# The later batches' layer-norm rows normalised on GpSimd instead of VectorE

## The chip, the cores and the metric

The kernel runs on one core of a Trainium2 chip. The metric is the device time of that core in microseconds. A core has five engines with a queue of instructions each: TensorE (PE in the rows; PEld is its weight load), VectorE (DVE), ScalarE (ACT), GpSimd (POOL) and SyncE (SP), which here only issues DMAs.

## The reference

Four batches of 512 rows by 512 columns go through an attention-like mixer and a feed-forward block, each behind a layer norm and with a residual. Cut to what is computed:

```
_layernorm(x) = (x - mean(x)) / sqrt(var(x) + 1e-5)

q, kv = (n @ W_q.T), (n @ W_kv.T)            # n = _layernorm(x), 16 heads of 32
qf, kvf = fft(q), fft(kv)                    # along each head
qf, kvf = qf / |qf|, kvf / |kvf|             # L2 norm of each head
kvf = cumsum(kvf, axis=1)                    # along the 512 rows of a batch
x = x + (ifft(qf * kvf).real @ W_o.T)

n2 = _layernorm(x)
gate = silu((n2 @ fp8(gate_w)) * gate_scale) # 512 -> 1536
up   = (n2 @ fp8(up_w)) * up_scale           # 512 -> 1536
x = x + ((gate * up) @ fp8(down_w)) * down_scale
```

## The kernel before, in words

A batch b (0 to 3) is four tiles t of 128 rows by 512 columns. The Fourier matrices are folded into the projection weights once. To keep precision with 16-bit matmuls, an activation is stored as a high part and a low part (the value less its high part), and both go through TensorE.

The first norm of a tile has these steps: `dve_stats1` (mean and variance), `dve_root0_head`, `act_root0`, `dve_root0_tail` (the factor 1/sqrt, for four tiles at once), `dve_xn` (line 1074: row less mean, times factor, a TENSOR_SCALAR of 128x512 f32 with two per-partition scalars, into one of two buffers `xn`), `act_xh` (line 653, the high part into `xs`), `pool_xl` (line 1603, the low part), and `sp_xT` (line 1709), two DMA transposes into `xT`. TensorE then runs `pe_qk(b, t, 0)` and `pe_qk(b, t, 1)` (line 370), 12 matmuls each.

The second norm: `dve_o` (residual and statistics), `dve_ln2_head`, `act_sqrt2`, `dve_ln2_tail` (four short instructions that end on semaphore `v_n2`), `dve_hn` (line 1213, the same form of TENSOR_SCALAR, into `qk[:, t, 1, :]`), `act_hT` (line 731, high part into `ks`), `dve_hT` (line 1218, low part), and `sp_hT` (line 1722), two DMA transposes into `hT`. `pe_gate_up(b, 0)` (line 470) waits for all eight transposes of its batch.

Every engine's order is written out by hand and an engine never passes a waiting instruction. The work of batch b's feed-forward block is interleaved with the mixer of batch b+1. On TensorE, `pe_qk(b+1, ...)` for seven of eight pieces stands at the seam between two feed-forward blocks, just ahead of `pe_gate_up(b, 0)`. The eight pieces of `pe_qk` share two PSUM banks in turn, so `pe_qk(2, 1, 0)` can't start until ScalarE has read the bank of `pe_qk(2, 0, 0)` (`act_qk`, lines 667 and 675; its last reader counts `a_cp`). The two buffers of `xs` are freed by the transposes that read them: `act_xh(b, t)` waits for the landing of tile t-2.

`dve_f` (line 1234) is the feed-forward's product of gate and up, `dve_fu` (line 1241) its low part.

ScalarE's order at the seam ahead of batch 1's feed-forward block, and SyncE's, are:

```
act_fu(e, 11)
act_hT(e, 1, 0) ... act_hT(e, 1, 3)
act_xh(e, 2, 3)
act_qk(e, 2, 0, 0)

sp_hT(e, 1, 1); sp_xT(e, 2, 3); sp_hT(e, 1, 2); sp_hT(e, 1, 3); sp_hT(e, 1, 0)
```

The rest, with the line numbers of the profile:

Of the kernel before, what the change touches and what calls it, by code (L numbers as in the profile page):

```python
# [10 lines left out]
ALU = mybir.AluOpType  # L11
# [4 lines left out]
NB = 4  # L16
NT = 4
# [74 lines left out]
def build(nc, x, w_q, w_kv, woT, gate_w, up_w, down_w, gs_d, us_d, ds_d, cst_d, cst2_d, id_d, out):  # L92
    ctx = ExitStack()
    with ctx:
# [3 lines left out]
        def sem(name):  # L98
            return ctx.enter_context(nc.semaphore(name))
# [61 lines left out]
        def bank(name):  # L161
# [136 lines left out]
        def xs_free(e, b, t):  # L298

            if 4 * b + t > 1:  # L300
                was_b, was_t = divmod(4 * b + t - 2, NT)
                e.wait_ge(d_xT[was_t], 32 * (was_b + 1))

        def x_low_done(b, t):
            return (v_xl, 1) if (b, t) == (0, 0) else (p_xl, 4 * b + t)
# [342 lines left out]

        def act_xh(e, b, t):

            e.wait_ge(v_xn, 4 * b + t + 1)
            xs_free(e, b, t)
            e.activation(xs[:, t % 2, 0, :], xn[:, t % 2, :], ACT.Copy).then_inc(a_xh, 1)  # L653

# [68 lines left out]

        def act_hT(e, b, t):

            e.wait_ge(v_hn, 4 * b + t + 1)
            if b == 0:
                e.wait_ge(s_tri, 4)
            else:
                e.wait_ge(d_zT[t], 32 * b)  # L730
            e.activation(ks[:, 0, t, :], qk[:, t, 1, :], ACT.Copy).then_inc(a_hT, 1)
# [549 lines left out]
        def vector_program(e):  # L1281
# [131 lines left out]
            dve_product(e, 1, 1)  # L1413
            dve_zl(e, 1, 0)
            dve_scale(e, 1, 2, 0)
            dve_xn(e, 2, 0)
            dve_f(e, 5)
            dve_round(e, 11)
            dve_fu(e, 4)
            dve_xn(e, 2, 1)  # L1420
            dve_round(e, 12)
            dve_f(e, 6)
            dve_scale(e, 1, 3, 1)
# [19 lines left out]
            dve_zl(e, 1, 3)  # L1443
            dve_o(e, 1, 1)
            dve_f(e, 11)
            dve_xn(e, 2, 2)
            dve_round(e, 17)
            dve_o(e, 1, 2)
            dve_fu(e, 10)
            dve_o(e, 1, 3)  # L1450
            dve_ln2_head(e, 1, range(NT))
            dve_ln2_tail(e, 1, range(NT))
            dve_hn(e, 1, 0)
            dve_hn(e, 1, 1)
            dve_hn(e, 1, 2)
            dve_xn(e, 2, 3)
# [7 lines left out]
            for b in range(1, NB):  # L1464
                nxt = b + 1
                if nxt < NB:
                    dve_sum(e, nxt, 0, 0)
                    dve_sum(e, nxt, 0, 1)
                if nxt == HALF:
                    dve_most(e, 0, 0)  # L1470
                if nxt < NB:
                    dve_sum(e, nxt, 1, 0)
                if nxt == HALF:
                    dve_most(e, 0, 1)
                if nxt < NB:
                    dve_sum(e, nxt, 1, 1)
                if nxt == HALF:
                    dve_most(e, 1, 0)
                if nxt < NB:
                    dve_sum(e, nxt, 2, 0)  # L1480
                if nxt == HALF:
                    dve_most(e, 1, 1)
                    dve_most(e, 2, 0)
                    dve_most(e, 2, 1)
                    dve_gus(e)
                dve_f(e, b * NI)
                dve_scale_out(e, b - 1, 0)
                dve_fu(e, b * NI)
                if nxt < NB:
                    dve_sum(e, nxt, 2, 1)  # L1490
                dve_scale_out(e, b - 1, 1)
                if nxt < NB:
                    dve_sum(e, nxt, 3, 0)
                dve_scale_out(e, b - 1, 2)
                dve_scale_out(e, b - 1, 3)
                if nxt < NB:
                    dve_sum(e, nxt, 3, 1)
                dve_f(e, b * NI + 1)
                if nxt < NB:
                    dve_norm_tail(e, nxt, range(NT))  # L1500
                    dve_scale(e, nxt, 0, 1)
                if b + 2 < NB:
                    dve_stats1(e, b + 2, 0)
                dve_fu(e, b * NI + 1)
                if nxt < NB:
                    dve_scale(e, nxt, 0, 0)
                    dve_scale(e, nxt, 1, 1)
                dve_f(e, b * NI + 2)
                if nxt < NB:
                    dve_product(e, nxt, 0)  # L1510
                dve_f(e, b * NI + 3)
                if nxt < NB:
                    dve_scale(e, nxt, 1, 0)
                dve_fu(e, b * NI + 2)
                if nxt < NB:
                    dve_zl(e, nxt, 0)
                    dve_scale(e, nxt, 2, 1)
                dve_f(e, b * NI + 4)
                if nxt < NB:
                    dve_scale(e, nxt, 2, 0)  # L1520
                    dve_product(e, nxt, 1)
                    dve_scale(e, nxt, 3, 1)
                dve_fu(e, b * NI + 3)
                if nxt == HALF:
                    dve_unit2(e)
                if nxt < NB:
                    dve_zl(e, nxt, 1)
                    dve_product(e, nxt, 2)
                dve_f(e, b * NI + 5)
                if nxt < NB:  # L1530
                    dve_o(e, nxt, 0)
                dve_fu(e, b * NI + 4)
                if nxt < NB:
                    dve_scale(e, nxt, 3, 0)
                dve_f(e, b * NI + 6)
                dve_fu(e, b * NI + 5)
                if nxt < NB:
                    dve_product(e, nxt, 3)
                    dve_zl(e, nxt, 2)
                    dve_zl(e, nxt, 3)  # L1540
                    dve_o(e, nxt, 1)
                    dve_o(e, nxt, 2)
                dve_f(e, b * NI + 7)
                if nxt < NB:
                    dve_o(e, nxt, 3)
                    dve_ln2_head(e, nxt, range(NT))
                dve_fu(e, b * NI + 6)
                if nxt < NB:
                    dve_ln2_tail(e, nxt, range(NT))
                    dve_hn(e, nxt, 0)  # L1550
                dve_f(e, b * NI + 8)
                if nxt < NB:
                    dve_hT(e, nxt, 0)
                if b + 2 < NB:
                    dve_stats1(e, b + 2, 1)
                if nxt < NB:
                    dve_hn(e, nxt, 1)
                dve_fu(e, b * NI + 7)
                if b + 2 < NB:
                    dve_stats1(e, b + 2, 2)  # L1560
                if nxt < NB:
                    dve_hn(e, nxt, 2)
                    dve_hT(e, nxt, 1)
                if b + 2 < NB:
                    dve_stats1(e, b + 2, 3)
                if nxt < NB:
                    dve_hn(e, nxt, 3)
                    dve_hT(e, nxt, 2)
                dve_f(e, b * NI + 9)
                if nxt < NB:  # L1570
                    dve_hT(e, nxt, 3)
                dve_fu(e, b * NI + 8)
                if b + 2 < NB:
                    dve_root0_head(e, b + 2, range(NT))
                dve_fu(e, b * NI + 9)
                if b + 2 < NB:
                    dve_root0_tail(e, b + 2, range(NT))
                    dve_xn(e, b + 2, 0)
                    dve_xn(e, b + 2, 1)
                dve_f(e, b * NI + 10)  # L1580
                dve_fu(e, b * NI + 10)
                if b + 2 < NB:
                    dve_xn(e, b + 2, 2)
                dve_f(e, b * NI + 11)
                dve_fu(e, b * NI + 11)
                if b + 2 < NB:
                    dve_xn(e, b + 2, 3)
            for t in range(3):
                dve_scale_out(e, NB - 1, t)
            dve_out_half(e)  # L1590
# [50 lines left out]
        def gpsimd_program(e):  # L1641
# [18 lines left out]
            pool_ks(e, 1, 1)  # L1660
            pool_product(e, 1, 0)
            pool_ks(e, 1, 2)
            pool_xl(e, 2, 0)
            pool_product(e, 1, 1)
            pool_product(e, 1, 2)
            pool_ks(e, 1, 3)
            pool_product(e, 1, 3)
            pool_xl(e, 2, 1)
            pool_xl(e, 2, 2)
            pool_xl(e, 2, 3)  # L1670

            for b in range(1, NB):
# [8 lines left out]
                if nxt < NB:  # L1681
# [5 lines left out]
                    pool_product(e, nxt, 2)  # L1687
                    pool_ks(e, nxt, 3)
                    pool_product(e, nxt, 3)
                if b + 2 < NB:  # L1690
                    pool_xl(e, b + 2, 0)
                    pool_xl(e, b + 2, 1)
                    pool_xl(e, b + 2, 2)
                    pool_xl(e, b + 2, 3)
            pool_out(e, NB - 1, 0)
# [245 lines left out]
```

## Time and profile before

| | us |
|---|---|
| median of 3 runs | 420.11 (420.07 to 420.39) |
| the profiled execution, its own time | 419.79 |
| its span, first to last instruction | 418.0 |
| TensorE busy | 408.8 (98% of the span) |
| VectorE busy | 297.4 (71%) |
| ScalarE busy | 193.2 (46%) |
| GpSimd busy | 108.2 (26%) |

The mean granted TensorE clock is 0.996 of full speed. The profile is of one execution; the 1.8 us between its time and its span lie outside the instructions. Its page gives busy time by engine and a chain of waits followed back from the last instruction. The share of that chain is 89% TensorE, 3% DMA, 3% VectorE, 2% ScalarE, 1% GpSimd.

### The profile page before, as it was taken

Reading aid. Unit: us, or ns where it says so; the run is one execution under the profiler, and the core shown is the slowest. Engines: PE = TensorE matmul, PEld = TensorE weight load, DVE = VectorE, ACT = ScalarE, POOL = GpSimd, SP = SyncE. Lnnn points to the kernel's source line nnn. Section 1 sums busy time; section 2 is a strip of 40 time slices with the busy share of each in tenths; the row PEclk is TensorE's granted clock in tenths of the full one; section 3 lists DMA queues with packets and bytes.
Section 4 is the critical chain, followed back from the end, with each engine's and each line's share of the span. In section 5 each row is a group of like instructions: output and inputs, shape, how many; then the busy total and the mean of one; then the engine's idle time right before and its main releaser. Section 6 shows DMA issues by size and latency. Waiting matters only on the chain.

```text
span 418.0 us, 5504 instructions
## 1 busy us (share of the span) xinstructions
PE 408.8 (98%) x1897; PEld 202.8 (49%) x1897; DVE 297.4 (71%) x514; ACT 193.2 (46%) x323; POOL 108.2 (26%) x114
## 2 busy tenths in 40 slices
PE   7999999999999999999999999999999999999994
PEld 3744454445555554454555555454444444444442
DVE  4998998999999699997984972167865854422234
ACT  3687756587736245445242563255442441131220
POOL 0133551015154137043541012032461001300003
PEclk9999999999999999999999999999999999999998
DMA  8986546600181143232112014411112051200002
GB/s 249 264 267 239 163 117 162 149 17 2 38 256 36 26 77 71 57 127 74 28 26 50 2 29 101 72 50 53 26 26 52 0 77 25 100 2 0 2 0 101
DMA packets 57547, 33.55 MB, mean 80 GB/s; under 512 B 49456, under 2 KB 49840, under 8 KB 57392
## 3 DMA queue, kind: packets, MB, share of 16 engines
q1 hardware_dynamic: 57088, 32.93, 30.3%
q8 instruction: 15, 0.25, 0.3%
q10 hardware_dynamic: 432, 0.28, 0.2%
q14 instruction: 12, 0.10, 0.1%
HBM read 17.44 MB, written 4.19 MB: 52 GB/s over the span
## 4 chain that ended last, share of the span: by engine, by line
PE 89%; DMA 3%; DVE 3%; ACT 2%; POOL 1%; SPq 1%; issue 1%; POOLq 0%; DVEq 0%
PE bd L488 20%; PE bu L470 19%; PE bg L470 19%; PE ba L370 14%; PE ba L415 8%; PE bd L370 3%; DMA h<-x_dram 1%; PE ba L388 1%; PE bd L415 1%; DMA hT<-w_q_dram 1%; PE bd L388 1%; PE bd L356 1%; PE bu L415 1%; POOL xs L1603 1%; PE bg L447 0%
## 5 line engine op out<-in xcount | busy, mean ns | idle before, releaser
L470 PE MATMUL bu<-hT,gu 128*128 128x512 f16 x384 | 90.7, 379 | 0.0
L470 PE MATMUL bg<-hT,gu 128*128 128x512 f16 x376 | 89.0, 379 | 0.0
L1234 DVE SCALAR_TENSOR_TENSOR ff<-bu,us,sl 128x512 f32<-128x512 f32 x48 | 35.9, 748 | 56.0 <-PE bu L470 52.8
L741 ACT ACTIVATE sl<-bg,gs 128x512 f32<-128x512 f32 x48 | 32.9, 686 | 78.0 <-PE bg L470 77.0
L370 PE MATMUL ba<-wf,xT 128*128 128x512 f16 x288 | 63.2, 379 | 0.0
L470 PEld LDWEIGHTS bu<-hT,gu 128*128 128x128 f16 x384 | 37.5, 98 | 45.5 <-DVE ff L1234 0.6
L470 PEld LDWEIGHTS bg<-hT,gu 128*128 128x128 f16 x376 | 35.6, 98 | 44.9 <-issue 4.1
L488 PE MATMUL bd<-dw,fu 128*128 128x512 f32 x192 | 51.1, 411 | 0.0
L1634 POOL TENSOR_TENSOR h<-ff,h 128x512 f32<-128x512 f32 x14 | 17.5, 1272 | 122.2 <-DVE ff L1265 122.2
L370 PEld LDWEIGHTS ba<-wf,xT 128*128 128x128 f16 x288 | 27.9, 98 | 34.1 <-issue 1.1
L488 PE MATMUL bd<-own,half 128*128 128x512 f16 x184 | 43.0, 379 | 0.0
L1603 POOL TENSOR_TENSOR xs<-xn,xs 128x512 f16<-128x512 f32 x15 | 20.4, 1369 | 79.7 <-ACT xs L653 79.7
L488 PEld LDWEIGHTS bd<-dw,fu 128*128 128x128 f32 x192 | 36.1, 188 | 9.6 <-DVE fu L1241 0.4
L1616 POOL TENSOR_TENSOR ks<-qk,ks 128x512 f16<-128x512 f32 x16 | 21.2, 1325 | 48.8 <-ACT ks L704 48.8
L415 PE MATMUL ba<-wo,qk 128*128 128x512 f16 x144 | 32.6, 379 | 0.0
L1050 DVE TENSOR_REDUCE S<-tu 128x16 f32<-128x512 f32 x32 | 21.5, 676 | 11.2 <-ACT tu L667 11.2
L488 PEld LDWEIGHTS bd<-own,half 128*128 128x128 f16 x184 | 17.9, 98 | 21.9 <-DVE half L1241 0.6
L1241 DVE TENSOR_TENSOR half<-ff,half 128x512 f16<-128x512 f32 x23 | 19.3, 839 | 11.9 <-ACT half L747 11.7
L667 ACT ACTIVATE tu<-ba 128x512 f32<-128x512 f32 x24 | 14.3, 594 | 22.2 <-PE ba L370 22.2
L1139 DVE TENSOR_TENSOR qk<-qk,sc 128x512 f32<-128x512 f32 x32 | 23.0, 736 | 0.2
L1241 DVE TENSOR_TENSOR fu<-ff,fu 128x512 fp32r<-128x512 f32 x24 | 20.8, 872 | 3.2 <-ACT fu L747 3.0
L747 ACT ACTIVATE half<-ff 128x512 f16<-128x512 f32 x23 | 14.3, 623 | 18.4 <-PE bd L488 13.2
(201 smaller groups left out, 524.3 us busy)
## 6 DMA issues: line engine op xcount, KB each, us to landing
h<-x_dram SPq DMA_DIRECT2D x16, 256.0 KB, 4.2
out_dram<-h SPq DMA_DIRECT2D x15, 256.0 KB, 2.0
hT<-w_q_dram SPq DMA_DIRECT2D x4, 256.0 KB, 5.0
gu<-w_kv_dram SPq DMA_DIRECT2D x4, 256.0 KB, 4.4
hT<-gate_w_dram SPq DMA_DIRECT2D x2, 512.0 KB, 3.5
hT<-up_w_dram SPq DMA_DIRECT2D x2, 512.0 KB, 5.6
gu<-woT_dram SPq DMA_DIRECT2D x1, 1024.0 KB, 5.1
hT<-down_w_dram SPq DMA_DIRECT2D x2, 512.0 KB, 4.9
```

Source lines behind the costliest of these rows:

```text
L370: m = e.matmul(ba[i][:, :], xT[:, b % 2, part_x, k, P * t:P * t + P], wf[:, w, part_w, k, :], start=k == 0 and part_x == part_w, stop=k == ...
L415: m = e.matmul(ba[i][:, :], src[:, part_p, P * j:P * j + P], wo[:, part_w, j, :], start=j == 0 and part_p == part_w, stop=j == KT - 1 and ...
L470: m = e.matmul(bk[:, :], gu[:, c, 4 * w + k, col:col + P], hT[:, b % 2, part, k, :], start=k == 0 and part == 0, stop=k == KT - 1 and part ...
L488: m = e.matmul(bd[t][:, :], fu_at(n)[:, part, P * t:P * t + P], (dw if n < HALF * NI else dw16)[:, i, :], start=i == 0 and part == 0, stop ...
L741: e.activation(sl[:, n % 2, :], bg[:, :], ACT.Silu, scale=gs[:, i:i + 1]).then_inc(a_silu, 1)
L1050: e.tensor_reduce(S[:, t, NH * w:NH * w + NH], v, AX.X, ALU.add).then_inc(v_sum, 1)
L1139: e.tensor_tensor(split_heads(qk[:, t, w, :]), split_heads(qk[:, t, w, :]), head_scale(t, w), ALU.mult).then_inc(v_kn if w else v_qn, 1)
L1234: e.scalar_tensor_tensor(out=ff[:, n % 2, :], in0=bu[:, :], scalar=(us if b < HALF else us2)[:, i:i + 1], in1=sl[:, n % 2, :], op0=ALU.mul ...
L1241: e.tensor_tensor(fu_at(n)[:, 1, :], ff[:, n % 2, :], high.bitcast(F32) if n < HALF * NI else high, ALU.subtract).then_inc(v_fu, 1)
L1603: e.tensor_tensor(xs[:, t % 2, 1, :], xn[:, t % 2, :], xs[:, t % 2, 0, :], ALU.subtract).then_inc(p_xl, 1)
L1616: e.tensor_tensor(ks[:, 1, t, :], qk[:, t, 1, :], ks[:, 0, t, :], ALU.subtract).then_inc(p_ks, 1)
L1634: e.tensor_tensor(hh, y_at(b, t), hh, ALU.add).then_inc(p_out, 1)
```

## The change

`dve_xn` of batches 2 and 3 (8 pieces) and `dve_hn` of batches 1, 2 and 3 (12 pieces) leave VectorE. GpSimd does the same arithmetic with the same form of instruction, in `pool_xn` and `pool_hn`; ScalarE waits on GpSimd's semaphores for them. Batches 0 and 1 of the first norm and batch 0 of the second stay on VectorE.

```diff
+        def xn_done(b, t):
+            return (v_xn, 4 * b + t + 1) if b < 2 else (p_xn, 4 * (b - 2) + t + 1)
+
+        def hn_done(b, t):
+            return (v_hn, t + 1) if b == 0 else (p_hn, 4 * (b - 1) + t + 1)
...
         def act_xh(e, b, t):
 
-            e.wait_ge(v_xn, 4 * b + t + 1)
+            e.wait_ge(*xn_done(b, t))
...
         def act_hT(e, b, t):
 
-            e.wait_ge(v_hn, 4 * b + t + 1)
+            e.wait_ge(*hn_done(b, t))
...
+        def pool_xn(e, b, t):
+            e.wait_ge(v_r1, 2 * roots_of(b, t) + 2)
+            e.wait_ge(*x_low_done(*divmod(4 * b + t - 2, NT)))
+            e.tensor_scalar(xn[:, t % 2, :], h[:, b % 3, t, :], mv1[:, t, 0:1], E1[:, 2, t:t + 1], ALU.subtract,
+                            ALU.mult).then_inc(p_xn, 1)
+
+        def pool_hn(e, b, t):
+            e.wait_ge(v_n2, 5 * n1_of(b, t) + 5)
+            e.wait_ge(p_ks, 4 * b + NT)
+            e.tensor_scalar(qk[:, t, 1, :], h[:, b % 3, t, :], mv2[:, t, 0:1], E2[:, 4, t:t + 1], ALU.subtract,
+                            ALU.mult).then_inc(p_hn, 1)
...
             pool_ks(e, 1, 2)
+            pool_xn(e, 2, 0)
+            pool_product(e, 1, 1)
+            pool_xn(e, 2, 1)
             pool_xl(e, 2, 0)
-            pool_product(e, 1, 1)
...
             pool_xl(e, 2, 1)
+            pool_xn(e, 2, 2)
+            pool_xn(e, 2, 3)
             pool_xl(e, 2, 2)
+            pool_hn(e, 1, 0)
+            pool_hn(e, 1, 1)
+            pool_hn(e, 1, 2)
+            pool_hn(e, 1, 3)
             pool_xl(e, 2, 3)
```

On VectorE the calls are dropped where they stood. In the loop over b the four `pool_hn(nxt, t)` stand behind the mixer's last `pool_product`, and `pool_xn(b + 2, t)` between the calls of `pool_xl(b + 2, t)`.

GpSimd ahead of the first seam (the end of batch 0's feed-forward block), before; xs is the low part of a tile, own the 16-bit copy of the down weights:

```order
L1616 TENSOR_TENSOR ks<-qk,ks 128x512 [waits act_ks]
L1625 TENSOR_TENSOR qk<-tu 128x16x16 [waits dve_U]
L1626 TENSOR_TENSOR qk<-tu 128x16x16
L1629 COPY qk<-tu 128x32 [waits pool_im,pool_re]
L1603 TENSOR_TENSOR xs<-xn,xs 128x512 [waits d_xT3,act_xh]
L1603 TENSOR_TENSOR xs<-xn,xs 128x512 [waits d_xT0,act_xh]
L1603 TENSOR_TENSOR xs<-xn,xs 128x512 [waits d_xT1,act_xh]
L1608 CAST own<-dw 128x1024 [waits dve_rd]
```

The same place now (1603 is `pool_hn` here, 1592 the low part, 1597 `pool_xn`):

```order
L1617 TENSOR_TENSOR ks<-qk,ks 128x512 [waits act_ks]
L1626 TENSOR_TENSOR qk<-tu 128x16x16 [waits dve_U]
L1627 TENSOR_TENSOR qk<-tu 128x16x16
L1630 COPY qk<-tu 128x32 [waits pool_im,pool_re]
L1592 TENSOR_TENSOR xs<-xn,xs 128x512 [waits d_xT3,act_xh]
L1597 TENSOR_SCALAR xn<-h,mv,E 128x512 [waits pool_xl,dve_r1] x2
L1592 TENSOR_TENSOR xs<-xn,xs 128x512 [waits d_xT0,act_xh]
L1603 TENSOR_SCALAR qk<-h,mv,E 128x512 [waits pool_ks,dve_n2] x4
L1592 TENSOR_TENSOR xs<-xn,xs 128x512 [waits d_xT1,act_xh]
L1609 CAST own<-dw 128x1024 [waits dve_rd]
```

Four pieces of the second norm now stand ahead of the low part of tile 3 of batch 2, and the last two pieces of the first norm ahead of that of tile 2.

VectorE at the same seam, before, from the last step of `dve_ln2_tail` on:

```order
L1125 SCALAR_TENSOR_TENSOR E<-E 128x4
L1213 TENSOR_SCALAR qk<-h,mv,E 128x512 x3
L1074 TENSOR_SCALAR xn<-h,mv,E 128x512
L1218 TENSOR_TENSOR ks<-qk,ks 128x512
L1213 TENSOR_SCALAR qk<-h,mv,E 128x512
L1218 TENSOR_TENSOR ks<-qk,ks 128x512
L1241 TENSOR_TENSOR fu<-ff,fu 128x512
L1218 TENSOR_TENSOR ks<-qk,ks 128x512 x2
```

And now (1226 is `dve_hT`, 1249 `dve_fu`):

```order
L1133 SCALAR_TENSOR_TENSOR E<-E 128x4
L1226 TENSOR_TENSOR ks<-qk,ks 128x512 x2
L1249 TENSOR_TENSOR fu<-ff,fu 128x512
L1226 TENSOR_TENSOR ks<-qk,ks 128x512 x2
```

Five TENSOR_SCALAR are gone from this stretch, and the five TENSOR_TENSOR that follow each other now have their inputs from GpSimd by way of ScalarE.

## Rows read from the trace of the kernel before

**Rows 1.** Page, part 1: busy us (share of the span) and instructions of each engine.
```profile
PE 408.8 (98%) x1897; PEld 202.8 (49%) x1897; DVE 297.4 (71%) x514; ACT 193.2 (46%) x323; POOL 108.2 (26%) x114
```

**Rows 2.** Stretch: us; busy PE, PEld, DVE, ACT, POOL; PE clock; DMA share; GB/s.
```profile
81.00:156.00 75.00, 75.00 (x341) 40.06 (x340) 68.79 (x106) 42.97 (x60) 23.75 (x22) 1.00 0.28 69
...
sum 327.00, PE 326.72 PEld 161.21 DVE 222.51 ACT 142.42 POOL 83.50; mean PE 81.68 PEld 40.30 DVE 55.63 ACT 35.60 POOL 20.88
```

**Rows 3.** Groups by form: count, then busy us, mean ns, idle before.
```profile
L1213 DVE TENSOR_SCALAR qk<-h,mv,E 128x512 f32<-128x512 f32 x16 | 8.5, 540 | 0.2
...
L1608 POOL CAST own<-dw 128x1024 f16<-128x1024 f32 x6 | 6.0, 1035 | 0.0
L1634 POOL TENSOR_TENSOR h<-ff,h 128x512 f32<-128x512 f32 x14 | 17.5, 1272 | 122.2 <-DVE ff L1265 122.2
```

**Rows 4.** Chain of waits at three seams: start us, us, what.
```profile
156.06 18.15 PE ba L370 x84
174.21 1.73 PE bg L470 x8
...
253.14 18.15 PE ba L370 x84
271.28 1.73 PE bg L470 x8
...
348.74 1.73 PE bg L470 x8
```

**Rows 5.** Timeline of VectorE, first seam: start us, us, instruction, idle before.
```profile
155.43 1.46 DVE L1213 TENSOR_SCALAR qk<-h,mv,E 128x512 f32<-128x512 f32 x3
...
157.87 0.54 DVE L1213 TENSOR_SCALAR qk<-h,mv,E 128x512 f32<-128x512 f32 x1
...
159.53 1.28 DVE L1218 TENSOR_TENSOR ks<-qk,ks 128x512 f16<-128x512 f32 x2
```

**Rows 6.** Timeline of ScalarE, first seam.
```profile
158.44 0.63 ACT L731 ACTIVATE ks<-qk 128x512 f16<-128x512 f32 x1 [0.76 <-DVE qk L1213]
...
159.97 0.59 ACT L675 ACTIVATE qk<-ba 128x512 f32<-128x512 f32 x1
```

**Rows 7.** Timeline of GpSimd, first and second seam.
```profile
159.67 2.16 POOL L1603 TENSOR_TENSOR xs<-xn,xs 128x512 f16<-128x512 f32 x1 [8.29 <-ACT xs L653]
...
246.75 1.16 POOL L1603 TENSOR_TENSOR xs<-xn,xs 128x512 f16<-128x512 f32 x1 [25.01 <-ACT xs L653]
```

**Rows 8.** Timeline of SyncE's queue, first seam, and landing of its transposes there.
```profile
161.64 2.53 SPq L1709 DMA_TRANSPOSE xT<-xs  x2
...
169.51 2.52 SPq L1722 DMA_TRANSPOSE hT<-ks  x2
DMA to landing us min/median/max: 2.5/2.5/2.5
```

**Rows 9.** Timeline of VectorE, ScalarE and SyncE's queue, second seam.
```profile
233.36 0.55 DVE L1213 TENSOR_SCALAR qk<-h,mv,E 128x512 f32<-128x512 f32 x1
...
240.22 0.53 DVE L1213 TENSOR_SCALAR qk<-h,mv,E 128x512 f32<-128x512 f32 x1
...
245.46 1.00 DVE L1074 TENSOR_SCALAR xn<-h,mv,E 128x512 f32<-128x512 f32 x2
...
256.82 0.59 ACT L675 ACTIVATE qk<-ba 128x512 f32<-128x512 f32 x1
...
246.75 2.50 SPq L1709 DMA_TRANSPOSE xT<-xs  x2
...
266.19 2.52 SPq L1722 DMA_TRANSPOSE hT<-ks  x2
```

**Rows 10.** Timeline of VectorE, ScalarE and SyncE's queue, third seam.
```profile
329.54 0.55 DVE L1213 TENSOR_SCALAR qk<-h,mv,E 128x512 f32<-128x512 f32 x1
...
333.24 0.69 ACT L741 ACTIVATE sl<-bg,gs 128x512 f32<-128x512 f32 x1 [1.73 <-PE bg L470]
...
335.19 11.58 SPq L1722 DMA_TRANSPOSE hT<-ks  x8
```

**Rows 11.** Timeline of ScalarE, where batch 2's first pieces move to.
```profile
120.84 0.69 ACT L741 ACTIVATE sl<-bg,gs 128x512 f32<-128x512 f32 x1 [6.19 <-PE bg L470]
```

More of the change, by code:

```diff
@@ L197, in build @@
         a_zh, v_zl = sem("act_zh"), sem("dve_zl")
+        p_hn, p_xn = sem("pool_hn"), sem("pool_xn")
         v_most, s_bound, a_bound, v_unit2, v_gus, p_dw = (
@@ L1415, in vector_program @@
             dve_scale(e, 1, 2, 0)
-            dve_xn(e, 2, 0)
             dve_f(e, 5)
@@ L1419, in vector_program @@
             dve_fu(e, 4)
-            dve_xn(e, 2, 1)
             dve_round(e, 12)
@@ L1445, in vector_program @@
             dve_f(e, 11)
-            dve_xn(e, 2, 2)
             dve_round(e, 17)
@@ L1452, in vector_program @@
             dve_ln2_tail(e, 1, range(NT))
[L1453 to L1456, printed above, removed]
             dve_hT(e, 1, 0)
-            dve_hn(e, 1, 3)
             dve_hT(e, 1, 1)
@@ L1549, in vector_program @@
                     dve_ln2_tail(e, nxt, range(NT))
-                    dve_hn(e, nxt, 0)
                 dve_f(e, b * NI + 8)
@@ L1555, in vector_program @@
                     dve_stats1(e, b + 2, 1)
-                if nxt < NB:
-                    dve_hn(e, nxt, 1)
                 dve_fu(e, b * NI + 7)
@@ L1561, in vector_program @@
                 if nxt < NB:
-                    dve_hn(e, nxt, 2)
                     dve_hT(e, nxt, 1)
@@ L1566, in vector_program @@
                 if nxt < NB:
-                    dve_hn(e, nxt, 3)
                     dve_hT(e, nxt, 2)
@@ L1577, in vector_program @@
                     dve_root0_tail(e, b + 2, range(NT))
-                    dve_xn(e, b + 2, 0)
-                    dve_xn(e, b + 2, 1)
                 dve_f(e, b * NI + 10)
                 dve_fu(e, b * NI + 10)
-                if b + 2 < NB:
-                    dve_xn(e, b + 2, 2)
                 dve_f(e, b * NI + 11)
                 dve_fu(e, b * NI + 11)
-                if b + 2 < NB:
-                    dve_xn(e, b + 2, 3)
             for t in range(3):
@@ L1689, in gpsimd_program @@
                     pool_product(e, nxt, 3)
+                    pool_hn(e, nxt, 0)
+                    pool_hn(e, nxt, 1)
+                    pool_hn(e, nxt, 2)
+                    pool_hn(e, nxt, 3)
                 if b + 2 < NB:
+                    pool_xn(e, b + 2, 0)
+                    pool_xn(e, b + 2, 1)
                     pool_xl(e, b + 2, 0)
+                    pool_xn(e, b + 2, 2)
                     pool_xl(e, b + 2, 1)
+                    pool_xn(e, b + 2, 3)
                     pool_xl(e, b + 2, 2)
```

## The prediction, made before the changed kernel was run

> **What bounds the kernel now.** I read the page's busy times first: TensorE is busy 98% of the span, VectorE 71%, GpSimd 26% [rows 1]. A share is a mean over stages, so I cut the span next: from 81 us, where the first feed-forward block begins, to 408 us TensorE is busy 326.7 of 327.0 us, at the full granted clock (2.4 GHz) [rows 2]. VectorE works 68.8 of 75 us in the densest stretch, yet TensorE never stands there. Every instruction that the change touches lies behind 81 us. So taking work off VectorE can return at most what TensorE stands idle there, 0.3 us. The question is only whether a piece that now comes from GpSimd arrives later than TensorE can bear. For that I took the chain of waits at the three seams, where TensorE goes from one feed-forward block by way of seven pieces of `pe_qk` to the next block [rows 4], and then the timelines of the other engines there, for how much room each link has.
>
> **What is removed.** 20 TENSOR_SCALAR at about 0.54 us [rows 3] (two of the first norm take 1.00 [rows 9]) are 10.8 us of VectorE time. Worth on the path: 0 to 0.3 us, by the paragraph above. I take 0.
>
> **What one piece costs on GpSimd.** No row shows GpSimd doing this form. From below: its one-input cast of 1024 columns takes 1035 ns, so half as many take about 0.52 us. From above: its two-input operation with f32 output over 512 columns takes 1272 ns on average, some of it stretched [rows 3]; the same with f16 output takes 1.16 us undisturbed [rows 7]. The new form has one input of 512 columns and two arithmetic steps. I take 0.85 us, between the two, and keep 0.52 to 1.27.
>
> The Trainium skill (GPSIMD Engine Reference, section Performance versus the Vector engine) gives about 1.8 cycles per element as the best case of a tight loop, 769 ns for 512 elements, and counts 2.6 for two inputs. The cast above, 1035 ns for 1024, is quicker than that rule allows for one input. With 0.77 in place of 0.85 the first-seam sum below would be about 0.3 us less.
>
> **GpSimd and VectorE disturb each other.** The low part `pool_xl` takes 1.16 us at 246.75, with VectorE on other kinds of work, but 2.16 us at 159.67 [rows 7], exactly while VectorE runs two `dve_hT` of two SBUF inputs, 1.28 us [rows 5]. The 1.0 us that GpSimd lost is nearly all of that time. So beside the pieces' own time I add 0.6 us (half of 1.28, rounded) for each two-input VectorE operation that falls between them.
>
> The Trainium skill (SBUF — State Buffer, section Who interferes with whom) states it as an exclusive lock: a VectorE instruction with two SBUF inputs and a GpSimd instruction that reads SBUF block each other for a whole instruction. The trace agrees, with 2.16 against 1.16 us. It speaks against this change: the consumers `dve_hT` fall right between the four new pieces.
>
> **First seam (156 to 174 us), where I expect the loss.** Before, the last of batch 1's four `dve_hn` runs 157.87 to 158.41 [rows 5]. Behind it ScalarE does four things without a gap: the high part at 158.44, `act_xh(2, 3)`, and the two reads of `pe_qk(2, 0, 0)`, of which the second runs 159.97 to 160.56 [rows 6]. That frees the bank for `pe_qk(2, 1, 0)`, which starts after 24 of the 84 matmuls, 156.06 + 24/84 x 18.15 = 161.25 [rows 4]. So there is room for 0.65 us: the last piece has to be done by about 159.05.
>
> Now the four pieces run one after another on GpSimd from 155.5 (the factor is ready at 155.43, where the first `dve_hn` started). With 0.85 each: 156.35, 157.2. Then `dve_hT(1, 0)`, whose high part ScalarE has ready at 157.0, gets in, 0.6: third piece 157.8 to 158.65; `dve_hT(1, 1)` to 159.25; fourth piece to 160.1. That is 1.05 us past 159.05. If `dve_fu(11)`, which stands directly behind `dve_hT(1, 1)`, gets in too, it is 1.65. I take 1.2 us, on TensorE's path in full, since TensorE has no idle time behind in which it could be made up.
>
> Both ends: with 0.52 a piece and two operations between, 155.5 + 2.1 + 1.2 = 158.8, hidden. With 1.27 and three between, 155.5 + 5.1 + 1.8 = 162.4, a loss of 3.3 us. Without any disturbance it would be 158.9 at 0.85 (hidden) and 1.5 us at 1.27.
>
> SyncE's queue runs beside it. Low part `pool_xl(2, 3)` now waits behind the four pieces, and its transpose is the second of the pair at 161.64, issued at 162.9. The last transpose issues at 170.8 and lands 2.5 later, 173.3 [rows 8], against 174.21 for the gate matmul [rows 4]: 0.9 us of room. Forecast: fourth piece 160.1, plus 1.2 for the two ScalarE steps, plus 1.16 to 2.16, so 162.5 to 163.5, late by 0 to 0.6. Hidden, the more so as TensorE comes 1.2 later.
>
> **Second seam (245 to 271 us).** Here `pool_xn(3, 0)` starts at 245.5, where `dve_xn` did. The low part of tile 0 waits for piece 1 too, since that stands ahead of it: it ends at 245.5 + 2 x 0.85 + 1.16 = 248.35, while the second transpose was issued at 248.0 (the pair starts at 246.75, 2.50 us) [rows 9]. SyncE's queue shifts by 0.35. From there it is a chain: `act_xh(3, 3)` waits for the landing of tile 1, and behind it the copy of `pe_qk(3, 0, 0)` ends at 257.41 [rows 9], against 253.14 + 5.19 = 258.33 where TensorE wants the bank [rows 4]: 0.9 of room. The last transpose issues at 267.45 and lands at 269.95, against 271.28: 1.3 of room. At 0.85 nothing is lost; at 1.27 the shift is 245.5 + 2.54 + 1.16 - 248.0 = 1.2, a loss of 0.3. The four `pool_hn(2, t)` are begun at 233.4 and done by some 238 at 0.85 with two disturbances; VectorE, which had them among other work, began its last at 240.22 [rows 9]. They cost nothing up to 1.27 (239.7).
>
> **Third seam (329 to 349 us).** SyncE starts its eight transposes at 335.19, behind the high part of tile 1, and that behind the silu at 333.24, which waits for TensorE [rows 10]. The high part of tile 1 needs two pieces, done by 331.3 at 0.85 and by 332.1 at 1.27, if they start at 329.54 as VectorE's first did. So the eight transposes start as before; they take 11.58 us, the last issues at about 345.5 and lands at 348.0, against 348.74 [rows 4]. I take 0.
>
> **Batch 2's early pieces (115 to 125 us)** take the place of low parts in GpSimd's order. ScalarE then stood idle for 6.19 us ahead of its next silu, waiting for TensorE [rows 11]: that idle time hides a high part that comes up to 2 us later. I take 0; without that cover it would be 1 to 2 us.
>
> **Sum.** 0 + 1.2 + 0 + 0 = 1.2 us on the profiled execution's 419.79: 421.0. The three runs' median lies 0.3 above that execution, so I predict 421.3, 0.3% slower.
>
> **The rivals.** First, hidden (not slower): a piece takes 0.6 us or less, or GpSimd's pieces and `dve_hT` don't hold each other up, so that the fourth piece is done by 159.05. For it: the cast's 0.52 for 512 columns, and 0.65 us of room. Against: the stretched row of 2.16. Time: 420.1. It decides at 0.88 a piece without disturbance and at 0.6 with it.
>
> Second, dear pieces: at 1.27 or more, 3.3 + 0.3 = 3.6 us, 423.7; at 1.5 about a microsecond and a half more. For it: VectorE's 0.54 [rows 3] is not far under its 0.64 for a two-input operation (1.28 for two [rows 5]), so a two-step piece need not be much cheaper than a two-input one on GpSimd. Against: the cast.
>
> Third, faster: VectorE's relief removes TensorE's small gaps, 0.3 us at most, 419.8. That can't be told from no change.
>
> **How the numbers follow.** About 0.2% (0.84 us) is what a measurement of this kernel can tell from no change; slower means above 420.95. Forecast case (0.7 to 2.2 us lost, 420.8 to 422.3): 0.42. Hidden: 0.36. Dear pieces: 0.20. Faster: 0.02. The forecast case has a small part below 420.95. Together slower 0.59, same 0.39, faster 0.02. The range goes from 419.9, below which only noise lies, to 424.3, which holds pieces of up to about 1.4 us.
>
> **What would show it.** The row of the new form on GpSimd: 0.85 us, or stretched ones of 1.4 beside short ones. ScalarE's high part of tile 3 at about 160.1 in place of 158.44, the copy behind it ending near 162.2, and a gap of TensorE ahead of the third piece of `pe_qk` at 161.3, of about 1 us, named after ScalarE. No gap at 258, 271 and 348. VectorE's busy time less by some 11 us, GpSimd's more by 17 to 20. A TensorE still busy without a gap at 161 would prove the first seam wrong; a gap ahead of a gate matmul would mean that SyncE's queue, not the bank, was the tighter link.

## The result and the profile after

The changed kernel takes 428.59 us (median of 5 runs, 428.27 to 429.41); before takes 420.07. The ratio is 1.0216, 95% interval 1.0201 to 1.023: 8.5 us slower. I had forecast slower, 421.3 us, in a range up to 424.3. The direction held, the size didn't: the loss is seven times the 1.2 us of the sum.

The page's busy times, the answer to [rows 1]:

```profile
PE 411.2 (96%) x1897; PEld 203.1 (48%) x1897; DVE 290.1 (68%) x494; ACT 193.0 (45%) x323; POOL 149.1 (35%) x134
```

VectorE is 7.3 us less busy, where I had forecast 11, and GpSimd 40.9 us more, where I had forecast 17 to 20. TensorE has the same instructions and is 2.4 us longer busy, the first hint that it ran some of them at a lower clock. The groups of the new form, which [rows 3] could not show:

```profile
L1603 POOL TENSOR_SCALAR qk<-h,mv,E 128x512 f32<-128x512 f32 x12 | 25.3, 2117 | 24.9 <-DVE E L1133 24.9
...
L1597 POOL TENSOR_SCALAR xn<-h,mv,E 128x512 f32<-128x512 f32 x8 | 18.0, 2251 | 3.9 <-DVE E L1075 3.6 <-POOL xs L1592 0.4
```

A piece takes 2.1 to 2.3 us on GpSimd, against 0.54 on VectorE. What TensorE waited for, in the table of waits (total us, times, longest):

```profile
PE ba L378 <- ACT qk L683: 6.2, 2, 4.7
```

Two stops, both ahead of the third piece of `pe_qk`, both for ScalarE's read of a bank. TensorE's timeline at the two seams, to be set against the unbroken 84 matmuls of [rows 4]:

```profile
155.92 5.35 PE L378 MATMUL ba<-wf,xT 128*128 128x512 f16 x24
165.95 14.76 PE L378 MATMUL ba<-wf,xT 128*128 128x512 f16 x60 [4.68 <-ACT qk L683]
180.55 1.89 PE L478 MATMUL bg<-hT,gu 128*128 128x512 f16 x8
...
260.13 5.34 PE L378 MATMUL ba<-wf,xT 128*128 128x512 f16 x24
266.98 13.12 PE L378 MATMUL ba<-wf,xT 128*128 128x512 f16 x60 [1.51 <-ACT qk L683]
279.94 1.89 PE L478 MATMUL bg<-hT,gu 128*128 128x512 f16 x8
```

Behind the first stop 60 matmuls take 14.76 us; behind the second the same 60 take 13.12. The stretches around the first (columns: us, then busy PE, PEld, DVE, ACT, POOL, granted clock, DMA share, GB/s) say why:

```profile
161.00:166.00 5.00, 0.32 (x3) 0.05 (x2) 2.56 (x5) 2.85 (x6) 3.74 (x3) 0.99 0.26 52
166.00:170.00 4.00, 4.00 (x12) 1.45 (x13) 3.01 (x3) 0.87 (x2) 4.00 (x5) 0.59 0.49 98
```

The granted clock is 0.59 of full speed on average in the 4 us after TensorE had stood 4.7 us; part of them ran at the lower level, 1.2 GHz. That costs 14.76 - 13.12 = 1.6 us. The producer's and ScalarE's timelines there, against [rows 5, 6]:

```profile
155.50 8.24 POOL L1603 TENSOR_SCALAR qk<-h,mv,E 128x512 f32<-128x512 f32 x4 [1.71 <-DVE E L1133]
```

```profile
163.78 0.63 ACT L739 ACTIVATE ks<-qk 128x512 f16<-128x512 f32 x1 [1.43 <-POOL qk L1603]
164.31 0.61 ACT L661 ACTIVATE xs<-xn 128x512 f16<-128x512 f32 x1
164.83 0.58 ACT L675 ACTIVATE tu<-ba 128x512 f32<-128x512 f32 x1
165.31 0.59 ACT L683 ACTIVATE qk<-ba 128x512 f32<-128x512 f32 x1
```

Four pieces in 8.24 us, the last high part at 163.78 where it was at 158.44, and the bank read at 165.9. One VectorE operation among them, for the question of disturbance:

```profile
160.33 0.69 DVE L1226 TENSOR_TENSOR ks<-qk,ks 128x512 f16<-128x512 f32 x1 [1.36 <-ACT ks L739]
```

The sum over the span (426.8 against 418.0, 8.8 us), read from the starts of TensorE's stretches: the third piece of `pe_qk` at the first seam begins 4.85 us later (165.95 against 161.10), the gate matmul behind it 6.5 (180.55 against 174.05; the lower clock added 1.65), a down matmul at 250.74 6.9, `pe_qk` at the second seam 7.15 (260.13 against 252.98), and the gate matmul behind that 8.8; behind it nothing is added. The 0.4 us at 250.74 come from the second norm's pieces too: that matmul waits for a `dve_fu` that stands behind a `dve_hT`, and this one had waited 0.70 us for ScalarE's high part of a GpSimd piece. (`e7_only_x3` below, without these pieces, has no such wait.)

### The profile page after: what moved, and what is told of

It reads as the page before. It is cut to its first block, busy times and chain, and to the rows that moved or that the text cites. A ratio compares the mean times of both kernels' runs of the same rounds, so it can differ in the third digit from the quotient of the medians.

```text
span 426.8 us, 5504 instructions
## 1 busy us (share of the span) xinstructions
PE 411.2 (96%) x1897; PEld 203.1 (48%) x1897; DVE 290.1 (68%) x494; ACT 193.0 (45%) x323; POOL 149.1 (35%) x134
## 4 chain that ended last, share of the span: by engine, by line
PE 68%; issue 9%; POOL 8%; DMA 4%; DVE 3%; ACT 3%; SPq 2%; POOLq 0%; ACTq 0%; DVEq 0%
PE bg L478 15%; PE bu L478 15%; PE bd L496 14%; PE ba L378 11%; PE ba L423 4%; POOL qk L1603 3%; PE bd L378 2%; DMA h<-x_dram 2%; POOL xs L1592 1%; PE bd L423 1%; PE ba L396 1%; DMA hT<-w_q_dram 1%; POOL qk L1626 1%; SPq L1726 1%; PE bd L396 1%
## 5 line engine op out<-in xcount | busy, mean ns | idle before, releaser
L378 PE MATMUL ba<-wf,xT 128*128 128x512 f16 x288 | 65.2, 386 | 6.3 <-ACT qk L683 6.2
L1603 POOL TENSOR_SCALAR qk<-h,mv,E 128x512 f32<-128x512 f32 x12 | 25.3, 2117 | 24.9 <-DVE E L1133 24.9
L1592 POOL TENSOR_TENSOR xs<-xn,xs 128x512 f16<-128x512 f32 x15 | 19.1, 1277 | 40.8 <-ACT xs L661 40.8
L1249 DVE TENSOR_TENSOR fu<-ff,fu 128x512 fp32r<-128x512 f32 x24 | 21.8, 917 | 6.1 <-ACT fu L755 6.0
```

What stands on the lines that cost most here:

```text
L378: m = e.matmul(ba[i][:, :], xT[:, b % 2, part_x, k, P * t:P * t + P], wf[:, w, part_w, k, :], start=k == 0 and part_x == part_w, stop=k == ...
L1249: e.tensor_tensor(fu_at(n)[:, 1, :], ff[:, n % 2, :], high.bitcast(F32) if n < HALF * NI else high, ALU.subtract).then_inc(v_fu, 1)
L1603: e.tensor_scalar(qk[:, t, 1, :], h[:, b % 3, t, :], mv2[:, t, 0:1], E2[:, 4, t:t + 1], ALU.subtract, ALU.mult).then_inc(p_hn, 1)
```

## The experiments

All but `after_again`, which is the changed kernel itself, are built from the kernel before by a list of the pieces that go to GpSimd; `e4_forms` has an empty list and a stretch behind the end. Ratios are to the kernel before on the same chip. Between executions the start of the program (up to the first seam) varies by about 1 us either way in all kernels, so differences under 1 us are read from the traces where they can be.

**Which pieces.** `e1_only_h1`: `ON_POOL_H = [(1, 0), (1, 1), (1, 2), (1, 3)]`, `ON_POOL_X = []`.

> Only the four second-norm pieces of batch 1 on GpSimd, everything else as before. Theory A (a piece takes 2.06 us on GpSimd, four in a row end at 163.7 where TensorE's bank bore 159.05, and the long stop lowers the clock behind it): a TensorE wait of 4.7 us ahead of the third piece of pe_qk and 1.8 us of slower matmuls behind it, so about 426.6 us, 6.5 over before. Rival B (the loss comes from the first-norm pieces, through the low parts and SyncE's transposes): within 1 us of before, 421 or less.

Measured: 427.11 us against 419.41, ratio 1.0178 (1.0156 to 1.02). Theory A holds, B falls. TensorE:

```profile
166.01 15.81 PE L385 MATMUL ba<-wf,xT 128*128 128x512 f16 x60 [4.93 <-ACT qk L690]
```

The same stop, 4.9 us, and a longer stretch of lower clock behind it: 2.7 us lost there by 15.81 against 13.12.

`e2_all_but_h1`: the other sixteen pieces.

> The other sixteen pieces on GpSimd, the four of batch 1's second norm back on VectorE. Theory A: no wait at the first seam, a wait of 1.5 to 1.9 us at the second, too short to lower the clock, and up to 0.6 us of small waits: 421.6 to 422.6 us. Rival B: most of the 8.5 us stays, 427 or more.

Measured: 422.14 against 419.41, ratio 1.0062 (1.0038 to 1.0087). No stop at the first seam, 1.50 us at the second. The sixteen pieces lose 2.7 us, as expected; the four of batch 1's second norm make more than two thirds of the whole. The two parts add to 10.4 us where the whole loses 8.5: the traces show 1.1 us more of lower clock in `e1_only_h1` than in the changed kernel, and 0.6 us in `e2_all_but_h1` at 313 us, most of it a wait for a DMA, which the changed kernel's trace lacks.

`e7_only_x3`: the four first-norm pieces of batch 3 alone.

> Only the four first-norm pieces of batch 3 on GpSimd. Theory (the second seam's loss is the low part of tile 0 behind two pieces, through SyncE's queue to the bank): the low part ends at 245.5 + 4.1 + 1.16 = 250.8 against an issue at 248.0, a shift of 2.8 less 0.9 of room, so a stop of 1.9 us ahead of the third piece of pe_qk for batch 3, 1.5 to 2 us over before. Rival (the loss of the second seam comes from the second-norm pieces ahead of it): none.

Measured: 421.72 against 419.75, ratio 1.0042 (1.0025 to 1.0059), with the stop of the second seam in full:

```profile
259.67 13.12 PE L385 MATMUL ba<-wf,xT 128*128 128x512 f16 x60 [1.51 <-ACT qk L690]
```

The stop at the second seam is these pieces' alone; the second-norm pieces ahead of them have no part in it. The 1.51 us are not all that TensorE loses there: in this execution it was 0.56 us ahead of before's times up to the seam, began `pe_qk` only 0.16 ahead (at 252.82, after a wait for a transpose) and its third piece 1.50 behind, so 2.1 us in all, where the formula had 1.9.

**Is the lower clock a consequence of the stop?** The changed kernel with fillers in the stop:

```diff
                 if nxt < NB:
                     pe_qk(e, nxt, 0, 0)
                     pe_qk(e, nxt, 0, 1)
+                if nxt == 2:
+                    pe_fill(e, FILL)          # 20 matmuls into bg, after a_silu >= NI
+                if nxt < NB:
                     pe_qk(e, nxt, 1, 0)
```

> The changed kernel with 20 filler matmuls of 128x512 (0.216 us each, 4.3 us in all, their result unused) ahead of the third piece of pe_qk for batch 2, where TensorE stood 4.7 us. If the slower matmuls behind the stop come from the stop itself, the granted clock stays at its upper level there and the time falls by 1.8 us to about 426.8. If the lower clock has another cause, or the fillers cost what they take, it is 428.6 or more.

`e3_fill` ran on another chip than the changed kernel: 427.16 against 419.41, ratio 1.018 (1.0154 to 1.0205). Its trace has the clock at 1.00 throughout the seam. I ran both once more on one chip, as `after_again` and `e3b_fill`.

> The changed kernel once more, on the chip of the three that follow, so that they can be set against it: 8.5 us over before, with TensorE stopped 4.7 us at the first seam, 1.5 at the second, and some 2 us of matmuls at the lower clock behind the first stop.

> The same kernel as e3_fill (20 filler matmuls in the stop of the first seam), beside the changed kernel on one chip. Theory (the stop lowers the clock behind it): granted clock 1.00 from 161 to 174, 60 matmuls in 13.0 us, and 1.8 to 2.8 us under the changed kernel, by how long the lower clock lasted there. Rival (the clock falls anyway or the fillers lengthen the stop): no less than the changed kernel.

Measured on that chip: the changed kernel 429.48 (ratio 1.0236, 1.0209 to 1.0263), with fillers 427.32 (1.0195, 1.0172 to 1.0217), 2.2 us less. The intervals overlap by a little, and the traces decide it: in the three that have this stop without fillers (the changed kernel twice and `e1_only_h1`) the clock falls, in both with fillers it doesn't. TensorE and the clock with fillers (the second row is cut at 170 us):

```profile
161.25 4.48 PE L462 MATMUL bg<-wo 128*128 128x512 f16 x20
166.10 4.06 PE L385 MATMUL ba<-wf,xT 128*128 128x512 f16 x18 [0.37 <-ACT qk L700]
```

```profile
166.00:170.00 4.00, 3.90 (x18) 1.78 (x19) 3.63 (x4) 2.11 (x5) 4.00 (x5) 1.00 0.49 98
```

TensorE resumes at the same moment as without them, and at full clock. From the start of `pe_qk` to the first gate matmul behind the seam the changed kernel on this chip loses 6.5 us to before, with fillers 4.9. Useless work in a stop that can't be avoided is worth 1.7 us here by the traces and 2.2 by the medians. Over all traces, stops of 1.5 and 2.4 us left the clock up, and those of 2.6, 3.7 and 4.7 were followed by the lower level.

**How many pieces does the first seam bear?** `e6_h1_last2`: tiles 2 and 3; `e5_h1_last1`: tile 3 only.

> Only the last two of batch 1's four second-norm pieces on GpSimd. Theory: they start at 155.5 and end at 159.6, 0.6 us past the 159.05 that TensorE's bank bears: a stop of 0.6 us, too short for the clock, 0.5 to 1.0 us over before. Rival (any piece on GpSimd costs its share of the loss): half of the four pieces' loss, 3 us or more.

Measured: 422.97 against 419.5, ratio 1.0088 (1.0063 to 1.0114). A miss between both: GpSimd and TensorE show

```profile
155.80 5.95 POOL L1637 TENSOR_SCALAR qk<-h,mv,E 128x512 f32<-128x512 f32 x2 [4.12 <-DVE E L1142]
```

```profile
163.96 13.12 PE L385 MATMUL ba<-wf,xT 128*128 128x512 f16 x60 [2.40 <-ACT qk L690]
```

Two pieces in 5.95 us, not 4.1. The first takes 2.34, the second 3.62, and VectorE shows why:

```profile
157.49 1.28 DVE L1237 TENSOR_TENSOR ks<-qk,ks 128x512 f16<-128x512 f32 x2
158.69 0.68 DVE L1260 TENSOR_TENSOR fu<-ff,fu 128x512 fp32r<-128x512 f32 x1
159.29 0.68 DVE L1237 TENSOR_TENSOR ks<-qk,ks 128x512 f16<-128x512 f32 x1
162.45 0.69 DVE L1237 TENSOR_TENSOR ks<-qk,ks 128x512 f16<-128x512 f32 x1 [2.48 <-ACT ks L746]
```

Four two-input operations run end to end to 159.97, and the second piece begins in their middle, at 158.14; it takes 1.54 us more than one alone. The bank's chain is right (155.80 + 5.95 = 161.75, less 159.05 and the 0.3 by which this execution started its seam later, is 2.4), the piece's price is not a constant: it depends on what VectorE is doing when the piece begins.

> Only the last of batch 1's four second-norm pieces on GpSimd: it can start at 155.5 and ends at 157.6, before VectorE's own did (158.4). Theory: nothing lost, within 0.2% of before. Rival (any piece costs its share): 1.5 us over before.

Measured: 421.38 against 419.75, ratio 1.0037 (1.0024 to 1.005). Another miss. (The profiled execution is the slowest of the five, 422.68, and its seam starts 1.0 us later than before's.) The seam is unbroken, but TensorE stops later, at the running sum of batch 2:

```profile
194.07 0.59 PE L403 MATMUL ba<-ks,tr 128*128 128x512 f16 x2 [1.69 <-POOL ks L1651]
```

VectorE's timeline at the seam, to be set against 159.53 in [rows 5], and GpSimd's low part, against 159.67 in [rows 7]:

```profile
160.12 1.22 POOL L1622 TENSOR_TENSOR xs<-xn,xs 128x512 f16<-128x512 f32 x1 [1.27 <-ACT xs L668]
160.25 1.64 DVE L1260 TENSOR_TENSOR fu<-ff,fu 128x512 fp32r<-128x512 f32 x1
161.81 2.96 DVE L1237 TENSOR_TENSOR ks<-qk,ks 128x512 f16<-128x512 f32 x2
```

Two low parts take 2.96 us where they took 1.28, beside GpSimd's casts of the weights. These began at 161.29, 0.5 us earlier than before and 1.5 earlier against the seam. The low part ahead of them takes 1.64 where it takes 0.68, beside GpSimd's `pool_xl`: before, VectorE's operation had begun first there and `pool_xl` took 2.16; here `pool_xl` began first and takes 1.22. VectorE has no idle time for the next 20 us and hands the delay to `pe_tri`. The test: hold the casts.

```diff
             if n == 0:
                 e.wait_ge(*rounded(17))
+                e.wait_ge(v_hT, 8)
```

> e5_h1_last1 (one piece on GpSimd, measured 0.37% over before) with the casts of the down weights on GpSimd held until VectorE's last low part of batch 1 is done. In e5_h1_last1 they began 0.5 us earlier than before, beside VectorE's two-input operations, which took 1.64 and 1.48 us each in place of 0.68; VectorE ran 2.5 us late and TensorE stopped 1.7 us at pe_tri(2, 0). Theory (GpSimd and VectorE block each other there, and VectorE has about 1 us of room behind the seam): no stop at pe_tri, within 0.2% of before. Rival (the loss is of the piece itself or of the start of the program): 0.3% over before as it was.

Measured: 420.16 against 419.67, ratio 1.0012 (1.0003 to 1.0021): within 0.2%, as expected, and TensorE's wait at `pe_tri` fell to 0.3 us. The interval doesn't reach 1, so a tenth of a per cent may be left. VectorE and GpSimd:

```profile
160.06 1.64 DVE L1260 TENSOR_TENSOR fu<-ff,fu 128x512 fp32r<-128x512 f32 x1
161.62 1.28 DVE L1237 TENSOR_TENSOR ks<-qk,ks 128x512 f16<-128x512 f32 x2
```

```profile
163.04 4.00 POOL L1644 CAST own<-dw 128x1024 f16<-128x1024 f32 x4 [1.89 <-DVE ks L1237]
```

The two low parts are back at 1.28. The one ahead of them is still at 1.64, as `pool_xl` still begins first: it was not the casts' doing, and the recorded theory was wrong to count it with them.

`e9_free`: `ON_POOL_H = [(3, 0), (3, 1), (3, 2), (3, 3)]`, `ON_POOL_X = [(2, 0), (2, 1)]`.

> The six pieces that by the traces have cover: the first norm of tiles 0 and 1 of batch 2, and the second norm of batch 3. Theory: no stop of TensorE, within 0.2% of before, 12.4 us of GpSimd's time and 3.2 us of VectorE's notwithstanding. Rival (disturbance of VectorE by the long pieces is felt everywhere): 1 us or more over before. Neither expects it faster.

Measured: 421.1 against 419.75, ratio 1.003 (1.0017 to 1.0042). Slower by a little more than I had said. Its trace is 1.1 us longer than before's and has both seams at before's times (155.87 and 252.92). It loses 0.43 us in two small gaps from 309 us on, between the second and the third seam, a stretch with none of the six pieces in it; `e6_h1_last2`, which moves nothing there either, loses a like amount at the same place. The other 0.7 us are behind the last matmul: the last output's DMA lands 3.3 us after its issue, where before's took 2.6. So in this execution no loss lies at a moved piece. Why the median of twelve is 1.3 us over before, no trace shows, and it stays open.

**Which link is the tight one?** `e8_reads_first` is the changed kernel with ScalarE in another order, and `e10_sums_first` has VectorE's reductions moved too:

```diff
             act_hT(e, 1, 0)
+            act_xh(e, 2, 3)
+            act_qk(e, 2, 0, 0)
+            act_qk(e, 2, 0, 1)
             act_hT(e, 1, 1)
             act_hT(e, 1, 2)
             act_hT(e, 1, 3)
-            act_xh(e, 2, 3)
...
             dve_hT(e, 1, 0)
+            dve_sum(e, 2, 0, 0)               # these two in e10_sums_first only
+            dve_sum(e, 2, 0, 1)
             dve_hn(e, 1, 3)
             dve_hT(e, 1, 1)
```

The same calls are dropped where they stood in the loop.

> The changed kernel with one edit on ScalarE: act_xh(2, 3) and both reads of the first pair of pe_qk stand ahead of the high parts of tiles 1 to 3, so that the bank is freed without waiting for GpSimd's four pieces. Theory (the bank behind ScalarE's queue is the link that stops TensorE): no stop ahead of the third piece, no lower clock; what is late next is the last landing of hT, near 175.2 against 174.2, so a loss of 1 to 1.6 at this seam, 1.5 to 2 at the second as before: 3 to 4 us over before, 423.1 to 424.1. Rival (the transposes behind the late pieces were as late as the bank): 6 us or more over before.

Measured: 426.91 against 419.5, ratio 1.0179 (1.0154 to 1.0204), 2.6 us under the changed kernel on the same chip but far from the 3 to 4 I had given. TensorE, and what ScalarE waited for:

```profile
154.80 10.53 PE L385 MATMUL ba<-wf,xT 128*128 128x512 f16 x48
167.95 9.63 PE L385 MATMUL ba<-wf,xT 128*128 128x512 f16 x36 [2.62 <-ACT qk L690]
```

```profile
166.81 0.60 ACT L682 ACTIVATE tu<-ba 128x512 f32<-128x512 f32 x1 [3.53 <-DVE S L1068]
```

The stop at the third piece is gone and stands at the fifth: ScalarE's next square waits for VectorE's reduction, which is queued behind the late low parts. The clock falls again (36 matmuls in 9.63 us; at full clock 7.9). At the first seam TensorE loses 4.5 us by this trace, where the changed kernel loses 6.5, and 1.0 more in a wait at `pe_tri` behind it.

> e8_reads_first with a second edit, on VectorE: the two reductions of the first pair of pe_qk stand ahead of the low parts of tiles 1 to 3. In e8_reads_first TensorE then stopped 2.6 us ahead of the fifth piece, since ScalarE's next square waited for them. Theory (the bank behind the queues of ScalarE and VectorE is the only tight link of the first seam beside the landings): no stop of 1 us or more in pe_qk there and no lower clock; the last landing of hT, some 19 us after the start of pe_qk by e8_reads_first's transposes against 18.15, costs about 1 us; second seam 1.5, small waits 0.6: 3 us over before. Rival (something else of the late pieces holds TensorE): 6 us or more.

Measured: 428.62 against 419.67, ratio 1.0218 (1.0204 to 1.0232): no gain over the changed kernel's 1.0216 and 1.0236, on other chips. (The profiled execution is the fastest of the five, 427.33.) All 84 matmuls run unbroken now, and the gate matmul behind them waits, with the lower clock behind the stop: eight matmuls in 3.30 us where they take 1.89.

```profile
155.83 18.30 PE L385 MATMUL ba<-wf,xT 128*128 128x512 f16 x84
177.88 3.30 PE L485 MATMUL bg<-hT,gu 128*128 128x512 f16 x8 [3.75 <-issue]
```

```profile
163.57 2.50 SPq L1778 DMA_TRANSPOSE hT<-ks  x2
166.17 2.52 SPq L1765 DMA_TRANSPOSE xT<-xs  x2
168.79 7.76 SPq L1778 DMA_TRANSPOSE hT<-ks  x6
```

The row names "issue", but the times are those of the landing: the last transpose issues at 168.79 + 7.76 - 1.27 = 175.3 and lands 2.5 later, 177.8. My theory that the bank is the only tight link falls. The late pieces hold TensorE by three ways one behind another (bank, reduction, landing), and taking one away shows the next. The size of the third is in part this edit's own: the high part of tile 1 now stood behind the reads on ScalarE, so SyncE's queue began at 163.57, where it began at 161.05 in the changed kernel. There its last transposes landed at 176.6 against the 174.07 at which 84 unbroken matmuls would have ended: by this estimate 2.5 of the 3.75 us measured here are due to the pieces alone.

**The piece by itself.** A stretch behind the last output of the kernel before, with VectorE idle, then beside a stream of VectorE's operations.

> The kernel before with a stretch added behind its last output: eight GpSimd instructions while VectorE is idle (two-step TENSOR_SCALAR with two pointers, one-step with a pointer, two-step with constants, one-step with a constant, two-step on 256 columns, copy, two-input subtract, two-step again), then three pieces and three two-input operations beside a VectorE stream of two-input operations, then the same beside VectorE's own TENSOR_SCALAR. Theory A: the two-step form takes 2.06 us alone, and the number of arithmetic steps sets it, so the one-step forms take about 1.1 and 256 columns 1.1. Rival: fetching the per-partition scalars is dear, so constants are quicker with two steps. Contention: if the two-input VectorE operations block GpSimd as the stretched row of before suggests, both forms are stretched beside them; by the changed kernel's rows (four pieces in 8.24 us with two-input operations between) only the two-input form is.

GpSimd's timeline, VectorE idle:

```profile
414.50 2.08 POOL L1683 TENSOR_SCALAR xT<-qk,mv,E 128x512 f32<-128x512 f32 x1
416.56 1.58 POOL L1694 TENSOR_SCALAR xT<-qk,E 128x512 f32<-128x512 f32 x1
418.10 1.94 POOL L1695 TENSOR_SCALAR xT<-qk 128x512 f32<-128x512 f32 x1
420.00 1.51 POOL L1696 TENSOR_SCALAR xT<-qk 128x512 f32<-128x512 f32 x1
421.49 1.24 POOL L1697 TENSOR_SCALAR xT<-qk,mv,E 128x256 f32<-128x256 f32 x1
422.66 0.62 POOL L1698 COPY xT<-qk 128x512 f32<-128x512 f32 x1
423.24 1.27 POOL L1686 TENSOR_TENSOR xT<-qk 128x512 f32<-128x512 f32 x1
...
427.45 7.83 POOL L1683 TENSOR_SCALAR xT<-qk,mv,E 128x512 f32<-128x512 f32 x3 [0.88 <-DVE wf L1715]
435.37 5.06 POOL L1686 TENSOR_TENSOR xT<-qk 128x512 f32<-128x512 f32 x3
453.36 6.81 POOL L1683 TENSOR_SCALAR xT<-qk,mv,E 128x512 f32<-128x512 f32 x3 [12.93 <-DVE wf L1719]
```

Two steps cost 2.08 us, one step 1.58; constants in place of pointers save 0.14 and 0.07. So the pointers are not what is dear: the second step is 0.4 to 0.5 us, and even one step is 0.9 to 1.0 more than a copy. (The second step is the subtraction, and the one-step forms only multiply; a lone subtraction was not run. Each form stands here once or twice in one execution.) Theory A had the time in proportion to the steps (1.1 for one), and that is wrong; for half the columns, 1.24, it was nearly right. The two-input operation, 1.27, which I had taken as the upper bound, is much cheaper than a one-input piece with two steps. Beside a dense stream of two-input operations a piece takes 2.6 (7.83 for three), and the two-input form 1.7; beside VectorE's own TENSOR_SCALAR a piece takes 2.3 (6.81 for three). VectorE's side, its stream undisturbed and against GpSimd's two-input form:

```profile
L1715 DVE TENSOR_TENSOR wf<-qk 128x512 f32<-128x512 f32 x16 | 11.1, 693 | 0.5
```

```profile
L1715 DVE TENSOR_TENSOR wf<-qk 128x512 f32<-128x512 f32 x3 | 4.9, 1634 | 0.1
```

## Why the prediction was right or wrong

**What bounds the kernel: right.** Nothing was won by 7 us less on VectorE; what counted was whether TensorE had to stand, and, what the prediction left out, at what clock it went on.

**What one piece costs on GpSimd: wrong, and this is the step that failed.** It took 0.85 us, with 1.27 as the upper bound; measured are 2.08 alone and 2.06 in the row of four. I bounded an operation that no row showed by its neighbours in the number of inputs, as though inputs were what costs. `e4_forms` shows that the form itself does: 1.5 to 1.6 us with one arithmetic step against 0.62 for a copy of the same size, and 0.4 to 0.5 more for the second step. The upper bound was no bound: nothing in the trace said that two inputs is the worst case.

**The first seam's chain: right, without the disturbance.** With 2.06 a piece it gives 155.5 + 8.24 = 163.74, less 159.05, 4.7 us; measured 4.68. The prediction's formula also added 0.6 for each of two or three VectorE operations, which would have made it 5.9 to 6.5; these terms were not there. `e1_only_h1` shows that these four pieces alone do it, by the bank behind ScalarE, as the prediction said.

**The lower clock behind the stop: not in the sum.** The prediction put it at nothing, without a word. It is 1.6 us in the profile of the changed kernel, 2.7 in `e1_only_h1`; `e3b_fill` shows that it comes from the stop.

**The second seam: right in mechanism.** The shift is 245.5 + 4.12 + 1.16 - 248.0 = 2.8, less 0.9 of room, 1.9; measured are 2.1 with the first norm's pieces alone, 1.51 of it as one stop, and 2.3 in the changed kernel. There 0.4 come ahead of the seam from the second norm's four pieces, which the prediction had at nothing up to 1.27 a piece.

**The third seam: right.** The gate matmul behind it moved by no more than the second seam's had: 8.8 us (357.39 against 348.58).

**The disturbance: a wrong rule.** The prediction added 0.6 us for each two-input VectorE operation between the pieces. In the changed kernel four such operations fall into the row of four pieces and add nothing: the pieces take 2.07 each and VectorE's operations 0.69. All of them began while a piece was under way. In `e6_h1_last2` the second piece began in the middle of a row of them and took 1.54 us more; both pieces together took 1.8 more, about 0.45 for each of the four operations, so 0.6 was not too small, but it counted the wrong thing. And disturbance works in the other direction, which the prediction did not follow: GpSimd's casts stretched two of VectorE's low parts from 1.28 to 2.96 us in `e5_h1_last1`, and `e11_last1_casts` took that away. The Trainium skill (SBUF — State Buffer, section Who interferes with whom) says that the order of issue decides which of the two engines is blocked. The low part `pool_xl` and VectorE's two-input operations bear it out: 2.16 us where VectorE's began first (159.53 against 159.67, before), and VectorE's at 1.64 where `pool_xl` did (160.12 against 160.25, `e5_h1_last1`). The page's exclusive lock, which the prediction cites, doesn't hold for the changed kernel's pieces: neither side is stretched there.

**Batch 2's early pieces: right.** The high part at 114.03 came 3.9 us later in the changed kernel (117.97), more than the 2 allowed for, and the 6.19 us of idle time hid it. TensorE's gate matmuls ahead of it start at 111.01 against 111.00, and `pe_qk` behind it at 155.92 against 155.91.

**The chances.** "Dear pieces", 0.20, was what happened, and dearer than its top. The range ended at 1.4 us a piece. Had the form's cost been left open to 2, as an operation with no row deserves, the same chains without disturbance would have given 4.45 + 1.76 = 6.2 us, 426.3; the rest to 428.6 is in the main the lower clock.

No version beat before. The best with any piece on GpSimd, `e11_last1_casts`, is 0.12% over it.

## What to carry to other kernels

Before moving an operation to an engine that has never run it in your trace, measure that form there alone; neighbours that differ in steps and inputs are no bound. On a kernel whose TensorE is gapless, look only for the room of each link ahead of it, and expect the next link just behind the first: here three stood within 3 us of each other. A stop of TensorE can cost more than its length, by the clock: here those of 2.6 us and more did.

## What the runs showed of the hardware that I had not expected

- GpSimd's TENSOR_SCALAR on 128x512 f32: 2.08 us with two steps, 1.58 with one, 1.94 and 1.51 with constants in place of per-partition scalars, against 0.62 for a copy and 1.27 for a two-input subtract.
- After TensorE had stood 4.7 us, the granted clock averaged 0.59 over the next 4 us; with 20 filler matmuls in the gap it stayed at 1.00. Stops of 1.5 and 2.4 us left it up, one of 2.6 was followed by the lower level.
- GpSimd's casts or two-input operations beside VectorE's two-input operations stretch these, from 0.64 to 1.48 us each in a pair and from 0.69 to 1.63. A two-step TENSOR_SCALAR under way on GpSimd is not stretched by single ones and doesn't stretch them (2.07 and 0.69 us); one that began within a row of four took 3.62.
